# Weight sums turned into rows by VectorE's block transposes, the softmax row scaled on ScalarE, and the fill reordered, in a fused two-layer graph kernel

## The reference

```python
qk = X @ Wqk; q, k = split(qk); v = X @ Wv                      # layer 0
agg = einsum('bij,bjd->bid', adj, k * mask[:, :, None])
w = mask * einsum('bid,bid->bi', q, agg) / sqrt(256)
x1 = layernorm(X + softmax(w, axis=1)[:, :, None] * v)
query, key, value = x1 @ Wq.T + bq, x1 @ Wk.T + bk, x1 @ Wv.T + bv   # layer 1
weight = adj * exp(einsum('bqd,bkd->bqk', query, key))
out = layernorm(x1 + (weight / weight.sum(2)) @ value)
```

## Time and profile before

| | |
|---|---|
| time, median of 3 runs | 292.46 us (292.09 to 293.44) |
| the profiled execution | 292.27 us, its span 290.5 us |
| TensorE matmul busy | 283.1 us, 97% of the span |
| VectorE busy | 253.4 us, 87% |
| ScalarE busy | 238.1 us, 82% |
| GpSimd busy | 217.3 us, 75% |
| granted TensorE clock, mean | 0.997 of full speed |
| chain that ended last | 95% of it on TensorE |

### The profile page before, as it was taken

One profiled execution on the slowest core, in us unless ns is written; L12 is line 12 of the kernel. 1 busy time (PEld: TensorE's weight loads), 2 busy tenths in 40 slices (PEclk: granted clock), 3 DMA queues, 4 the chain that ended last, 5 costly groups with the idle time before them and its releaser, 6 DMA issues.

```text
span 290.5 us, 7075 instructions
## 1 busy us (share of the span) xinstructions
PE 283.1 (97%) x1984; PEld 263.6 (91%) x1984; DVE 253.4 (87%) x783; ACT 238.1 (82%) x568; POOL 217.3 (75%) x269
## 2 busy tenths in 40 slices
PE   8999999999999999999999999999999999999991
PEld 7879999999999999999999999999999999999990
DVE  1478999999989999999998999899999999999775
ACT  4555779899888989988898998889899888987863
POOL 1466987778898777789877778987777897777332
PEclk9999999999999999999999999999999999999998
DMA  7931234233333432333442333434333343210113
GB/s 239 324 108 37 92 93 128 92 92 98 108 123 127 127 95 86 95 104 126 127 123 97 87 97 102 127 127 126 93 88 97 102 127 127 90 57 14 58 38 108
DMA packets 19165, 31.26 MB, mean 108 GB/s; under 512 B 2128, under 2 KB 6608, under 8 KB 19152
## 3 DMA queue, kind: packets, MB, share of 16 engines
q1 hardware_dynamic: 19152, 31.11, 34.6%
HBM read 22.71 MB, written 8.39 MB: 107 GB/s over the span
## 4 chain that ended last, share of the span: by engine, by line
PE 95%; DVE 2%; issue 1%; POOL 0%; POOLq 0%; DVEq 0%; ACT 0%; ACTq 0%
PE ps L889 25%; PE ps L890 24%; PE ps L891 24%; PE ps L992 10%; PE ps L972 5%; PE ps L1112 1%; PE ps L940 1%; PE ps L912 1%; PE ps L1117 1%; PE ps L997 1%; PE ps L1126 1%; PE ps L951 1%; DVE stats L620 0%; PE ps L1133 0%; DVE x_sum L639 0%
## 5 line engine op out<-in xcount | busy, mean ns | idle before, releaser
L889 PE MATMUL ps<-w_hi,xt_hi 128*128 128x512 f32 x124 | 49.4, 398 | 0.0
L890 PE MATMUL ps<-w_lo,xt_hi 128*128 128x512 f32 x124 | 48.5, 391 | 0.0
L891 PE MATMUL ps<-w_hi,xt_lo 128*128 128x512 f32 x124 | 48.3, 390 | 0.0
L372 POOL TENSOR_TENSOR edge_lo<-edge,edge_hi 128x256 fp32r<-128x256 f32 x29 | 21.4, 739 | 34.6 <-ACT edge_hi L541 34.6
L461 ACT ACTIVATE x<-x_sum,shift,rstd 128x256 f32<-128x256 f32 x60 | 32.9, 595 | 14.7 <-POOL shift L386 14.7
L305 POOL TENSOR_TENSOR x1b<-x,bv_all 128x512 f32<-128x512 f32 x31 | 39.9, 1287 | 2.9 <-DVE x L822 2.0
L359 POOL TENSOR_TENSOR xt_lo<-xt_raw,xt_hi 128x512 fp32r<-128x512 f32 x31 | 40.0, 1292 | 1.8 <-ACT xt_hi L443 1.8
L383 POOL TENSOR_TENSOR rstd<-var_eps,minus_half 128x4 f32<-128x4 f32 x31 | 31.5, 1017 | 8.5 <-DVE var_eps L798 8.5
L889 PE MATMUL ps<-x1t_hi,at_hi 128*128 128x256 f32 x124 | 37.4, 302 | 0.0
L366 POOL TENSOR_TENSOR x_lo<-x_raw,x_hi 128x512 fp32r<-128x512 f32 x28 | 36.1, 1289 | 0.0
L889 PE MATMUL ps<-wv_hi,x1t_hi 128*128 128x258 f32 x124 | 35.6, 287 | 0.0
(11 more groups left out here) (165 smaller groups left out, 909.6 us busy)
## 6 DMA issues: line engine op xcount, KB each, us to landing
xt_raw<-xt_pairs SPq DMA_DIRECT2D x32, 256.0 KB, 2.7
x_raw<-x_pairs SPq DMA_DIRECT2D x32, 256.0 KB, 2.7
out_pairs<-x SPq DMA_DIRECT2D x31, 256.0 KB, 2.0
adjt<-adjt_pairs SPq DMA_DIRECT2D x32, 129.0 KB, 2.0
p<-params SPq DMA_DIRECT2D x1, 770.0 KB, 6.8
p<-params SPq DMA_DIRECT2D x1, 512.0 KB, 3.8
p<-params SPq DMA_DIRECT2D x1, 256.0 KB, 4.2
out_pairs<-x SPq DMA_DIRECT2D x2, 128.0 KB, 1.8
```

Source lines behind the costliest of these rows:

```text
L889: nc.tensor.matmul(out, s_hi, m_hi, start=first, stop=False)
L890: nc.tensor.matmul(out, s_hi, m_lo, start=False, stop=False)
L891: return nc.tensor.matmul(out, s_lo, m_hi, start=False, stop=last)
```

## The change

Weight rows: for pairs 3 to 30 VectorE itself turns `w_col`, now 32 columns wide and cleared at the start, into a row `w_row` in SBUF, by four block transposes behind the weight sums; `row_max` follows them at once, and TensorE no longer transposes for these pairs. Softmax row: for the same pairs ScalarE scales the row, between the two halves of z; VectorE takes only the reciprocal, between its two x2 sums. The score bias goes to ScalarE, behind the high part of the values. The high part of x is made one slot later, for pair t+3 behind the high part of xt. The scores run k outside and g inside, so that their first half waits only for the first half of z. The statistics of x2 move from the end of slot t-1 to slot t, behind those of x1. In the fill, the weight sums of pair 1 come ahead of the low part of the folded matrix (`low_at` in the new code, the same two instructions), and the first half of the first x1 is normalised by VectorE, the second by ScalarE.

In the diff, `bias_scores` and `scale_row` are ScalarE's, `norm_first_half`, `transpose_w` and the statistics VectorE's, `scores` and `queries` TensorE's.

```diff
+        def w_rows(r):
+            return w_row_ps(r) if by_tensor(r) else w_row[0:2, :]
                     if r == 0:
                         pool.wait_ge(bv_loaded, 16)
+                        pool.wait_ge(first_half_normed, 1)
+            nc.gpsimd.memset(w_col[:, :], 0.0)
...
+            def bias_scores(u):
+                act.wait_ge(score_exp_done, u)
+                nc.scalar.activation(score_bias[:, :], val_ps[:, :, DIM], ACT.Identity, bias=s_bias[:, 0:1])\
+                    .then_inc(score_bias_done, 1)
+            def scale_row(u, r):
+                act.wait_ge(inv_sum_done, u + 1)
+                nc.scalar.activation(p_row_ps(r)[0:2, :], exp_row_ps(r), ACT.Copy, scale=inv_sum[:, 0:1])\
+                    .then_inc(p_row_done, 1)
...
-                if r == 0:
-                    split_x(4, 4)
+                if exists(t + 3) and r + 3 >= SPLIT:
+                    split_x(t + 3, r + 3)
...
                 if exists(t) and r != 0:
                     act.wait_ge(z_done, t + 1)
-                    bias_z(z)
+                    bias_half(z, 0, z_half_copied)
+                    if exists(t + 2) and not by_tensor(r + 2):
+                        scale_row(t + 2, r + 2)
+                    bias_half(z, 1, z_copied)
...
-                if exists(t + 4) and r + 4 > SPLIT:
-                    split_x(t + 4, r + 4)
+                    if r != DRAIN:
+                        bias_scores(t)
...
+            def norm_first_half():
+                dve.wait_ge(rstd_done, 1)
+                nc.vector.tensor_scalar(x1[0][:, graph(0)], x1_sum[0][:, graph(0)], neg_mean[:, 0, 0:1], rstd[1][:, 0, 0:1],
+                                        ALU.add, ALU.mult).then_inc(first_half_normed, 1)
...
+            def transpose_w(u, r):
+                for g in range(2):
+                    dve.wait_ge(w_done[g], u + 1)
+                dve.wait_ge(row_exp_done, u)
+                for b in range(0, NODES, BLOCK):
+                    block = nc.vector.transpose(w_row[:, b:b + BLOCK], w_col[b:b + BLOCK, :])
+                block.then_inc(w_row_done, 1)
...
                     both_stats(0, x1_sum[(r + 1) % 2]).then_inc(stats1_done, 1)
+                if exists(t - 2):
+                    dve.wait_ge(x2_done, t - 1)
+                    both_stats(1, x2[(r - 2) % 4]).then_inc(stats2_done, 1)
...
-                if r == -1:
-                    dve.wait_ge(at_hi_done, 1)
-                    nc.vector.tensor_tensor(wv1_lo[:, :, DIM], at_ps[:, :, DIM], wv1_hi[:, :, DIM].bitcast(F32), ALU.subtract)
-                    nc.vector.tensor_tensor(at_lo[:, :, :], at_ps[:, :, 0:DIM], at_hi[:, :, :].bitcast(F32), ALU.subtract)\
-                        .then_inc(at_lo_done, 1)
                 if exists(t + 2):
                     for g in range(2):
                         weight(t + 2, r + 2, g)
+                    if not by_tensor(r + 2):
+                        transpose_w(t + 2, r + 2)
+                        row_max(t + 2, r + 2)
...
                         if g == 1 and exists(t + 2):
-                            row_max(t + 2, r + 2)
+                            if by_tensor(r + 2):
+                                row_max(t + 2, r + 2)
+                            else:
+                                invert_sum(t + 2)
...
-                if exists(t - 1):
+                if r == DRAIN:
                     dve.wait_ge(x2_done, t)
                     both_stats(1, x2[(r - 1) % 4]).then_inc(stats2_done, 1)
...
-                        nc.vector.tensor_scalar(p_row_ps(r + 2)[0:2, :], exp_row_ps(r + 2), inv_sum[:, 0:1], None, ALU.mult)\
-                            .then_inc(p_row_done, 1)
                         dve.wait_ge(p_row_done, t + 3)
-                if exists(t) and r != DRAIN:
-                    bias_scores(t)
...
-            def scores(out, zs, xs):
-                for g in range(2):
-                    for k in range(HALVES):
+            def scores(u, out, zs, xs):
+                pe.wait_ge(z_half_copied, u + 1)
+                for k in range(HALVES):
+                    if k == 1:
+                        pe.wait_ge(z_copied, u + 1)
+                    for g in range(2):
...
-                    queries(x1t_hi, x1t_lo, (t + 2, r + 2) if exists(t + 2) and r > 0 else None)
+                    queries(x1t_hi, x1t_lo, (t + 2, r + 2) if r > 0 and by_tensor(r + 2) else None)
```

More of the change, by code:

```diff
@@ L87, in build @@
         agg = sb("agg", [128, 2, DIM])
-        w_col = sb("w_col", [128, 2])
+        w_col = sb("w_col", [128, BLOCK])
+        w_row = sb("w_row", [BLOCK, NODES])
         neg_max = sb("neg_max", [2, 1])
@@ L161, in build @@
         xt_hi_done, agg_copied, x1t_copied, z_copied = sem("xt_hi_done"), sem("agg_copied"), sem("x1t_copied"), sem("z_copied")
+        z_half_copied = sem("z_half_copied")
         row_exp_done, val_copied, score_exp_done = sem("row_exp_done"), sem("val_copied"), sem("score_exp_done")
@@ L456, in split_adjm, with norm @@
                 nc.scalar.copy(adjm_hi[r % 2][:, :], adjm[r % 2][:, :]).then_inc(adjm_hi_done, 1)
-            def norm(out, in_, layer, r, done, half_done=None):
+            def norm(out, in_, layer, r, done):
                 for g in range(2):
@@ L463, in norm @@
                                                 scale=rstd[r % 2][:, layer, g:g + 1])
-                    if half_done and g == 0:
-                        last.then_inc(half_done, 1)
                 last.then_inc(done, 1)
@@ L472, in exp_scores, with bias_half @@
                 last.then_inc(score_exp_done, 1)
-            def bias_z(to):
-                for m in range(HALVES):
-                    last = nc.scalar.activation(to[:, m, :], z_ps[:, m, :], ACT.Identity, bias=z_bias[:, m:m + 1])
-                last.then_inc(z_copied, 1)
+            def bias_scores(u):
+                act.wait_ge(score_exp_done, u)
+                nc.scalar.activation(score_bias[:, :], val_ps[:, :, DIM], ACT.Identity, bias=s_bias[:, 0:1])\
+                    .then_inc(score_bias_done, 1)
+            def bias_half(to, m, done):
+                nc.scalar.activation(to[:, m, :], z_ps[:, m, :], ACT.Identity, bias=z_bias[:, m:m + 1]).then_inc(done, 1)
+            def bias_z(to):
+                bias_half(to, 0, z_half_copied)
+                bias_half(to, 1, z_copied)
+            def scale_row(u, r):
+                act.wait_ge(inv_sum_done, u + 1)
+                nc.scalar.activation(p_row_ps(r)[0:2, :], exp_row_ps(r), ACT.Copy, scale=inv_sum[:, 0:1])\
+                    .then_inc(p_row_done, 1)
             def normed_out(u, n):
@@ L569, in slot @@
                         act.wait_ge(x1b_done, t)
-                    norm(x1[(r + 1) % 2], x1_sum[(r + 1) % 2], 0, r, x1_done,
-                         first_half_normed if r == -1 else None)
+                    if r == -1:
+                        nc.scalar.activation(x1[0][:, graph(1)], x1_sum[0][:, graph(1)], ACT.Identity,
+                                             bias=shift[1][:, 0, 1:2], scale=rstd[1][:, 0, 1:2]).then_inc(x1_done, 1)
+                    else:
+                        norm(x1[(r + 1) % 2], x1_sum[(r + 1) % 2], 0, r, x1_done)
                 if exists(t + 2):
                     act.wait_ge(row_max_done, t + 3)
-                    nc.scalar.activation(exp_row_ps(r + 2), w_row_ps(r + 2), ACT.Exp, bias=neg_max[:, 0:1],
+                    nc.scalar.activation(exp_row_ps(r + 2), w_rows(r + 2), ACT.Exp, bias=neg_max[:, 0:1],
                                          accum_out=exp_sum[:, 0:1]).then_inc(row_exp_done, 1)
@@ L608, in weight @@
             def weight(u, r, g):
+                if r == 0:
+                    dve.wait_ge(consts_ready, 1)
                 dve.wait_ge(agg_copied, u + 1)
@@ L670, in normed_x1, with low_at @@
                 last.then_inc(x1_done, 1)
+            def norm_first_half():
+                dve.wait_ge(rstd_done, 1)
+                nc.vector.tensor_scalar(x1[0][:, graph(0)], x1_sum[0][:, graph(0)], neg_mean[:, 0, 0:1], rstd[1][:, 0, 0:1],
+                                        ALU.add, ALU.mult).then_inc(first_half_normed, 1)
+            def low_at():
+                dve.wait_ge(at_hi_done, 1)
+                nc.vector.tensor_tensor(wv1_lo[:, :, DIM], at_ps[:, :, DIM], wv1_hi[:, :, DIM].bitcast(F32), ALU.subtract)
+                nc.vector.tensor_tensor(at_lo[:, :, :], at_ps[:, :, 0:DIM], at_hi[:, :, :].bitcast(F32), ALU.subtract)\
+                    .then_inc(at_lo_done, 1)
             def bias_scores(u):
@@ L760, in drain, with invert_sum @@
                                             ALU.add, ALU.mult).then_inc(last_out_done, 1)
+            def transpose_w(u, r):
[5 more added lines that the diff above has]
+                block.then_inc(w_row_done, 1)
+            def invert_sum(u):
+                dve.wait_ge(row_exp_done, u + 1)
+                nc.vector.reciprocal(inv_sum[:, :], exp_sum[:, :]).then_inc(inv_sum_done, 1)
```

(23 more changed lines are left out.)

## The result

The changed kernel takes 300.46 us (median; 300.17 to 301.49) against 292.51 for the kernel before (292.09 to 293.44): 1.0275 times as long, 95% interval 1.0248 to 1.0301. The forecast was 298.2, the range 293.0 to 302.0: slower, as forecast, by 7.95 us where 5.9 were forecast. The profiled execution has a span of 298.3 us (before 290.5). Some 0.4 us of the difference lies outside the span: the time of a run exceeds its span by 1.75 to 1.85 us in the kernel before and by 2.17 to 2.23 us in the changed one. The forecast has no term for this, and no run here shows what it is. In all profiles of this document TensorE's mean granted clock is 0.993 to 0.998, half a per cent from lowest to highest, so the 2.7% between the kernels are not the clock's.

What follows compares the result with a forecast made beforehand. TensorE, busy 97%, was taken to bound the kernel at 8.486 us a slot; the change makes a VectorE-GpSimd loop set 8.72. 292.27 - 0.2 + 6.1 - 0.36 (fill) + 0.4 (end) = 298.2 us, range 293.0 to 302.0.

Steps and rivals of the forecast that it cites:

- The deciding step: VectorE's moved x2 statistics add 0.62 us to the VectorE-GpSimd turn of 8.01, making 8.63, over TensorE's 8.38.
- The first loop: VectorE-GpSimd turn from `x1b` through held `edge`, x1 statistics, variance, `x_lo` and `adjm_lo` to `x1b`: 8.63 us with moved statistics.
- the second loop: From x1 statistics through weight sums, block transposes, row scaling, `adjm_hi`, `adjm_lo` and `x1b` back: 7.93 to 8.79 us.
- TensorE's saving: 28 weight transposes dropped from TensorE, 0.11 us each, 3.1 us in all; TensorE's slot falls from 8.486 to 8.38.
- the rival in which TensorE keeps the pace: `edge` gets through without waiting for `x1b`, so the whole saving comes: 288.8 us; chance 0.14.
- The fill: Earlier weight sums of pair 1 gain 0.36 us, bounds 0 to 0.5; VectorE's x1 normalisation hides beside TensorE's aggregate.
- The end: Slot 29 has both second-layer statistics on VectorE: 0 to 0.62 us more, 0.4 taken.
- 0.35 us of TensorE a slot: Sign of being right: TensorE waits some 0.35 us a slot, before scores and aggregate; its share falls to about 94%.
- signs of being wrong: `edge` at 0.42 and slot 8.38; GpSimd waiting for `adjm_hi` much over 0.1 us; or block transposes over 0.3 each.
- The block transposes of w: Rival: GpSimd's `x_lo` holds them on VectorE; slot grows by about 1.25 us, time about 331; chance 0.06.
- the time of 295.9: Skill-based estimate: block transposes from SBUF 0.26 us cheaper, second loop 8.53, slot 8.63, whole kernel 295.9 us.
- The loop felt only in part: Rival: `edge` sometimes goes before `x1b` starts; mean slot some 8.55, time 293.8 us; chance 0.10.

Runs made afterwards that it cites:

- b_stats_moved: Kernel before with only the statistics of x2 moved between those of x1 and `val_lo`: 298.21 us, 1.0190 of the kernel before.
- p_fill_scalar: Changed kernel with the exponential of the scores in PSUM and the first half of the first x1 normalised on ScalarE again: 291.06 us, 0.9951 of the kernel before.
- p_norm_free: Changed kernel with the exponential in PSUM; GpSimd's `xt_lo` of pair 2 waits until VectorE has normalised that first half of x1: 291.38 us, 0.9962.
- a_exp_psum: Changed kernel with the exponential of the scores written to PSUM in steady slots, so `edge` has one SBUF input: 291.76 us, 0.9970 of the kernel before.
- a_stats_back: Changed kernel with the statistics of x2 again behind the x2 sums at the end of a slot: 291.82 us, 0.9977 of the kernel before.

## Why the prediction came out as it did

**The deciding step was right.** The first loop was worked out at 8.63 with the statistics in it; alone it measured 8.685 (`b_stats_moved`). Of the second, through the block transposes, `adjm_hi` and `adjm_lo`, the bounds were 7.93 to 8.79; with both loops the slot is 8.749, against 8.72 taken. The traces show that the second is the one that ends last: `adjm_lo` starts 0.08 after `adjm_hi` ends in all 28 slots of the changed kernel (157.34 and 157.26 in the slot shown above), and 0.52 to 0.55 after it in all but the first two slots of `b_stats_moved`, which has no block transposes of w. So the first loop makes most of the loss and the second adds some 0.06. That the second loop makes this 0.06 was read from the traces and not tried by a run of its own.

The profiled execution took 300.53 us, 2.3 more than the forecast of 298.2. The slot, mis-sized by 0.03, is 0.7 of it, the fill 1.0, the end 0.1, and 0.5 lies outside the span.

**TensorE's saving was put too high.** The forecast took 0.11 us a transpose. Where TensorE sets the pace, steps fall from 8.47 to 8.40 or 8.41: 0.07. The query products with the transpose among them take 1.53 and without it 1.43, so 0.10 at its place, but the value products behind them take 1.46 in place of 1.44. The starts of its two neighbours gave the gap at its place and not what the products behind it regain. So the rival in which TensorE keeps the pace, 288.8, was out of reach by more than the loop: with the loop cured the kernels take 291.1 to 291.8.

**The fill failed.** The forecast was -0.56 up to the scores of slot 2 (-0.2 for two transposes, -0.36 for the earlier weights). It measured +0.42, of which 0.12 is the later start of the profile (11.92 against 11.80). The step that failed is the sentence that the normalisation on VectorE hides beside the aggregate. It is a `tensor_scalar` with one SBUF input, of the kind that the earlier trace rows show held by GpSimd, and GpSimd starts `xt_lo` at 17.57, just when it is issued (17.54). The prediction had read exactly this hold for `neg_mean` and not asked which new instruction it would meet. TensorE then waits 0.25 for x1:

```profile
19.04 0.66 PE L1018 MATMUL ps<-ident,x 128*128 128x128 f32 x4 [0.25 <-DVE x L699]
```

Nor was there 0.36 to win without it. The weights do come earlier: TensorE transposes those of pair 1 5.65 after the first weight transpose in place of 5.93, and waits 0.21 for them in place of 0.47. But `p_fill_scalar`, 0.21 ahead of the kernel before at the scores of slot 0 (13.08 against 13.29 after the first weight transpose), gives it back at the next step, where TensorE waits for the row of pair 2:

```profile
27.06 0.30 PE L992 MATMUL ps<-ident,p_row 128*128 128x128 f32 x1 [0.22 <-DVE p_row L898]
```

In `p_norm_free` the later `xt_lo` delays the projection of pair 2, which was the rival named there: ahead by 0.28 at the transposes of x1 (6.71 against 6.99), it is behind by 0.08 at that projection (7.43 against 7.35).

**The end had nearly the right size for a wrong reason.** +0.54 was measured and +0.4 forecast, as the price of two statistics in slot 29. `a_exp_psum` has both in slot 29 too, and from the scores of slot 28 to the end of its span it takes 289.4 - 262.08 = 27.32, against 27.28 before. The end is longer where the last slots start with a late loop, and not for the extra instruction: from the scores of slot 28 to the next it takes 9.63 in the changed kernel, 9.05 in `a_exp_psum`, 9.03 before.

**The signs.** `edge` at 0.7 to 1.1, ending 0.3 behind `x1b`: right. 0.35 us of TensorE a slot, before scores and aggregate: right in size and place (8.749 - 8.405 = 0.34; 0.10 at the scores, 0.2 before the aggregate, the rest in the value and aggregate products), but the view of waits doesn't list it, and the share stayed at 97% where 94% was forecast. In the slot shown the transposes are put down as busy until 157.65 + 0.60 = 158.25, behind the start of the aggregate that waits, so the stall before it counts as busy.

`x1b` every 8.63 to 8.79: right (8.74 to 8.77 in the steady slots). Four weight transposes on TensorE: right. Of the signs of being wrong none came: GpSimd waits for `adjm_hi` by 0.1 at most, and a block transpose of w takes 0.2.

**The rivals.** The block transposes of w are not held. In all 28 slots they take 0.84 to 0.85 for four beside GpSimd's `x_lo`, and are done before it is over:

```profile
154.14 1.29 POOL L371 TENSOR_TENSOR x_lo<-x_raw,x_hi 128x512 fp32r<-128x512 f32 x1
```

```profile
154.31 0.84 DVE L803 STREAM_TRANSPOSE w_row<-w_col 32x32 f32<-32x32 f32 x4
```

So that rival falls. The rule of the Trainium skill that spoke against it ("SBUF — State Buffer", section "Who interferes with whom": two SBUF inputs, or `tensor_scalar`, copies and casts with both port pairs, contend with GpSimd) agrees with the cases compared here: 0.78 against 0.42 for `edge`, 1.45 against 0.40 for the `tensor_scalar` of the fill, no hold of the block transposes. Whether that `tensor_scalar` ran with both port pairs no run shows. The other page, "VectorE: DVE Perf Modes", section "The TRN2 errata — SBUF-src ops pay a fixed extra latency per instruction", was not borne out: by it the four from SBUF would be 0.26 cheaper than those from PSUM, and they take 0.84 against 0.87 (before: 0.86). So the time of 295.9 that followed from it did not come. The loop felt only in part fell too: `edge` averages 925 ns and is held in every slot. (By the prediction's own sums `edge` would have had to be ready 8.12 - 7.30 = 0.82 sooner for it, not 0.7; this changes nothing.)

## What to carry to other kernels

Before an instruction is moved within an in-order queue, find the loops between engines that pass through its new place and compare each loop's turn, not the engine's sum, with the slot: here 0.62 us moved inside VectorE's queue, with its sum unchanged, cost 5.65 us. An instruction that a neighbour engine can hold turns such a chain into a closed loop; putting one operand into PSUM opened it. And once a hold has been found in the profile, every new instruction of the same kind has to be checked against what the other engine runs at that moment.

## What was not expected of the hardware

- A `tensor_scalar` with one SBUF input and two scalars per partition, 128x256, issued when GpSimd was starting a `tensor_tensor`, took 1.45 us, and 0.40 when GpSimd waited for it.
- VectorE's 32x32 block transposes cost nearly the same from SBUF (0.84 for four) as from PSUM (0.85 to 0.87), and were not held by the GpSimd `tensor_tensor` that ran beside them.
- TensorE's share of busy time was 97% both where it set the pace and where it lost 0.34 us in every slot.
- In `a_stats_back`, `a_exp_psum` and `p_norm_free` the step from slot 4 to 5 takes 8.68 or 8.69, 0.27 more than its neighbours; in `p_fill_scalar` it takes 8.42. In the three, the stretch from the transposes of x1 to the aggregate takes 0.57 or 0.58 there in place of 0.36, and GpSimd's `adjm_lo` waits 0.2 to 0.5 for `adjm_hi`. What makes `adjm_hi` late in this one slot is open.
